# ScalarE makes each scan step's decay half a step later in its order

## The reference, cut to what matters

```
def step(ht, inp):
    x_t, dt_t, B_t, C_t = inp
    dA = jnp.exp(dt_t[..., None] * A)
    dB = dt_t[..., None] * B_t[:, None, :]
    ht = dA * ht + dB * x_t[..., None]
    y_t = jnp.sum(ht * C_t[:, None, :], axis=-1)
    return (ht, y_t)
```

## Time and profile before

| what | us |
|---|---|
| median of 3 runs (lowest, highest) | 2696.54 (2693.64, 2705.16) |
| the profiled execution, its own time | 2710.37 |
| its span | 2708.3 |
| busy: PE, DVE, ACT, POOL | 2271.3 (84%), 1850.7 (68%), 1767.2 (65%), 1738.4 (64%) |

### The profile page before, as it was taken

The page is one execution under the profiler, slowest core; times in us unless marked ns, Lnnn a source line. Parts: engine busy times, 40 slices in busy tenths (PEclk is TensorE's granted clock), DMA queues, the critical chain, the costliest instruction groups (busy, mean ns, idle before and its releaser), DMA issues.

```text
span 2708.3 us, 38199 instructions
## 1 busy us (share of the span) xinstructions
PE 2271.3 (84%) x13192; PEld 1417.2 (52%) x13192; DVE 1850.7 (68%) x2832; ACT 1767.2 (65%) x3278; POOL 1738.4 (64%) x1416
## 2 busy tenths in 40 slices
PE   5777879999688889799989898989888988987781
PEld 4444557775444456455644465546544644554351
DVE  5778544543246786687578766876777667788888
ACT  3556534446277876788677867785887677766762
POOL 1000254425757997788788879876987797655565
PEclk9888989999899999999989998999999999998895
DMA  4000258874555676555665475447543844476776
GB/s 158 24 20 6 88 156 237 235 219 77 102 110 120 129 154 155 110 115 122 162 122 103 111 167 115 100 104 172 111 100 84 191 105 86 94 172 151 172 183 143
DMA packets 282032, 344.50 MB, mean 127 GB/s; under 512 B 66159, under 2 KB 211504, under 8 KB 281840
## 3 DMA queue, kind: packets, MB, share of 16 engines
q0 software_dynamic: 84080, 175.67, 34.7%
q1 hardware_dynamic: 175248, 144.83, 18.2%
q10 hardware_dynamic: 22512, 21.57, 2.4%
HBM read 198.26 MB, written 26.80 MB: 83 GB/s over the span
## 4 chain that ended last, share of the span: by engine, by line
PE 26%; POOL 15%; issue 11%; DVE 10%; ACT 9%; DMA 1%; POOLq 0%; DVEq 0%; SPq 0%; ACTq 0%
POOL arena L1661 6%; PE bank L1913 4%; PE bank L1944 4%; POOL acc_sb L1639 4%; DVE bank L1536 4%; POOL arena L1667 3%; POOL arena L1677 2%; PE bank L1739 2%; PE bank L1786 2%; PE bank L1779 2%; PE bank L1836 2%; PE bank L1798 2%; ACT Pr L1043 2%; DVE arena L1502 1%; ACT bank L1160 1%
## 5 line engine op out<-in xcount | busy, mean ns | idle before, releaser
L1661 POOL TENSOR_TENSOR arena<-arena 128x512 f32<-128x512 f32 x512 | 874.3, 1785 | 18.2 <-DVE arena L1527 9.5
L1639 POOL DMA_INDIRECT acc_sb<-ybuf,slot_idx x256 | 422.5, 1650 | 132.6 <-DMA ybuf<-arena 60.8
L1252 DVE TENSOR_REDUCE negmax<-bank 128x1 f32<-128x512 f32 x512 | 339.8, 680 | 240.8 <-PE bank L1779 239.2
L1160 ACT ACTIVATE bank<-arena,A_sb 128x512 f32<-128x512 f32 x512 | 353.4, 694 | 149.8 <-DVE arena L1541 131.2
L1043 ACT ACTIVATE Pr<-bank,negmax 128x512 f32<-128x512 f32 x512 | 358.5, 700 | 135.1 <-DVE negmax L1252 133.6
L1667 POOL TENSOR_TENSOR arena<-arena 128x512 f32<-128x512 f32 x192 | 297.5, 1550 | 231.5 <-DVE arena L1536 231.2
L1536 DVE TENSOR_TENSOR_SCAN bank<-bank,arena 128x512 f32<-128x512 f32 x320 | 390.0, 1219 | 67.1 <-ACT bank L1160 61.2
L1786 PE MATMUL bank<-ident,Pr 128*128 128x128 f32 x2048 | 341.1, 291 | 79.2 <-ACT PT L1025 77.5
L1786 PEld LDWEIGHTS bank<-ident,Pr 128*128 128x128 f32 x2048 | 229.1, 145 | 317.6 <-ACT PT L1025 181.1
L1025 ACT COPY PT<-bank 128x512 f32<-128x512 f32 x512 | 303.3, 592 | 128.6 <-PE bank L1786 101.0
L1779 PE MATMUL bank<-Kp,Qp 64*128 64x512 f32 x1024 | 301.5, 666 | 70.9 <-ACT Pr L1043 59.2
(11 more groups left out here) (216 smaller groups left out, 3773.7 us busy)
## 6 DMA issues: line engine op xcount, KB each, us to landing
arena<-arena POOLq DMA_DIRECT2D x255, 512.0 KB, 5.3
arena<-bc_dram SPq DMA_DIRECT2D x256, 256.0 KB, 3.8
ybuf<-arena ACTq DMA_DIRECT2D x64, 256.0 KB
arena<-in_w_gate SPq DMA_DIRECT2D x64, 128.0 KB
arena<-in_w_up SPq DMA_DIRECT2D x64, 128.0 KB
arena<-in_w_down SPq DMA_DIRECT2D x64, 128.0 KB
arena<-in_X SPq DMA_DIRECT2D x8, 512.0 KB, 8.4
s_sb<-in_X SPq DMA_DIRECT2D x8, 512.0 KB
```

The costliest lines, as they stand in the source:

```text
L1160: act.activation(bank[DECAY[g % 2]][:, :], dt_sb[:, size_slot(b, cb), :], ACT.Exp, scale=A_sb[:, cb, n:n + 1]).then_inc(ssm_decay, 1)
L1252: dve.tensor_reduce(negmax[:, m % RING_STAT:m % RING_STAT + 1], bank[m % RING_S_ATT][:, :], AX.X, ALU.max, negate=True).then_inc(att_max, 1)
L1639: pool.indirect_dma_start(acc_sb[:, i, :], None, ybuf, bass.IndirectOffsetOnAxis(ap=slot_idx[:, b * TILES + i, k:k + 1], axis=0), bounds_c ...
L1661: pool.tensor_tensor(st_sb[:, g % RING_S, :], u_sb[:, size_slot(b, cb), :], B_sb[:, load % RING_BC, :], ALU.mult).then_inc(ssm_input, 1)
```

## The change

The method `decay` of ScalarE becomes `ssm_step` itself, and its `ssm_mid` goes. Before, decay g + 1 was written in `ssm_mid(g)`, in the middle of step g (and decay 0 at step 0). Now decay g is written at the start of step g. The conditions it waits for are the same.

```
                 ins.then_inc(ssm_soft, 1)
 
             def ssm_step(self, g):
-                if g == 0:
-                    self.decay(0)
-
-            def ssm_mid(self, g):
-
-                self.decay(g + 1)
-
-            def decay(self, g):
                 if g < NB * SCAN:
                     b, cb, n, _ = ssm_place(g)
                     w.wait_ge(ssm_dt, len(SIZE_PARTS) * b + PART_OF[cb] + 1)
```

## The result

| | median us | lowest, highest | runs |
|---|---|---|---|
| before | 2696.26 | 2691.47, 2705.16 | 9 |
| after | 2714.65 | 2712.0, 2728.55 | 9 |

The ratio is 1.0069, with a 95% interval of [1.0053, 1.0086]: the change makes the kernel 18.4 us slower, more than the 0.5% that the prediction took as the bound of what can be told. The time lies inside the range of 2684 to 2727; the likeliest case, no change, did not come.

What follows compares the result with a forecast made beforehand. PE was taken to bound tree stretches, VectorE the last stretch, and no single engine attention. The terms +1 + 2 + 7 - 7 gave +3 us, a median of 2699.5, said as 2700, with a range of 2684 to 2727.

Steps and rivals of the forecast that it cites:

- no change: Whole kernel: the time stays within 0.5%, 2683 to 2710 us; chance some 0.45.
- slower rival: Attention: VectorE stands in line behind the late decay, so row maxima and GpSimd's product are late; 2727 us, chance 0.36.
- The sum, +3: Whole kernel: the four parts, +1 + 2 + 7 - 7, in us.
- Part 1: Tree stretches of batches 3, 4 and 5: six more table loads at 1.28 us, mostly covered; +1 us, bounds 0 and 7.7.
- the worked place: Trees of batch 5: two more loads make a silu late and cost PE 0.3 us.
- Part 2: Last stretch: eight decays fall behind a silu pair and stall scans; +2 us, bounds -2 and +15.
- Part 3: Attention: scans wait longer for the later decay, 54 us on VectorE, an eighth taken; +7 us, bounds 0 and +27.
- Part 4: Mainly attention: most of ScalarE's 60.9 us idling for VectorE before decays goes; -7 us, bounds 0 and -30.
- its mark: Outside the last stretch: scans' waits for the decay rise from 62.3 us to 90 or more.
- I am wrong if attention stretches grow by over 3 us each: Attention: the prediction's own sign of failure, by which VectorE's line behind late decays would be the story.
- The faster rival: ScalarE's idling for the product by C held up PE; 2676.5 us if half goes through, 2686.5 if a third; chance 0.19.
- the banks fix the decay's time whatever the order says: Whole kernel: the two banks set when a decay runs, so the order changes nothing; 2697.5 us, chance 0.10.

Runs made afterwards that it cites:

- e5: Kernel before with only three decays (steps 148, 212, 276) made later, enough to bring the six more table loads; ratio 0.9995.
- e3: Kernel before with decays later only in the tree stretches of the first six batches (111 decays, 183 table loads); ratio 1.0017.
- e4: Kernel before with decays later only in the last stretch, from scan step 409 on (103 decays); ratio 1.0018.
- e2: Kernel before with decays later only in the attention stretches (298 decays); ratio 1.0034.
- e7: Kernel before with decay g + 1 at the start of step g, half a step earlier; ratio 1.0111.
- f3: Changed order, with a third decay buffer in SBUF and an input ring of eight slots instead of ten; ratio 1.0421 against the kernel before.
- f2: Kernel before, order kept, with a third decay buffer in SBUF and an input ring of eight slots instead of ten; ratio 1.0341.
- e6: Decay g in the middle of step g, a whole step later than in the kernel before; ratio 1.0677.
- f1: Kernel before with an input ring of eight slots instead of ten, still two decay banks; ratio 0.9990.
- e1: The changed kernel itself, unedited, built and timed again against the kernel before; ratio 1.0071.

## Why the prediction was off, step by step

The measured time lies in the range only because the range reached up to the slower rival. The sum, +3, was 15 us short, and no change was the likeliest case.

**Part 1, table loads (+1).** The loads alone cost nothing that can be told in the time (e5). At the worked place PE idled 0.57 us for 0.3 foretold. By length the three stretches grew by 5.2 us in e5, five times the term, which the other stretches of that execution gave back.

**Trees without loads: no term.** The sum had nothing for the other decays in the tree stretches, since PE is full there. e3 measures the trees at +4.6 us, loads included, and the scans' waits for decays in them grew by 42.3 us (61.1 to 103.4). PE being full 62.27 of 63 us in one stretch is not PE full in all: between their scans the six tree stretches of before have PE busy 86 to 93% of the time. The waits had been there to see: summed by stretch, 61.1 of the 62.3 us in which scans waited for decays before lie in tree stretches. Whether the +4.6 is these decays or the loads is open, as said with e5.

**Part 2, last stretch (+2).** The mechanism was right, down to the place (0.80 us for 0.9) and to the waits (30.6 us, foretold between 22 and 35). The size was not: e4 has +4.9, from six decays and not eight. The working gave "+5 if VectorE carries all of it", and it does, as an engine busy 86% of the stretch would; I took 2 for what earlier trees might give back, and no row had shown that they would.

**Part 3, attention, the later decay (+7).** Its working was not what happened. It put 54 us of added waits on the 36 scans that waited already and took these to be in attention; only two of them are, with 1.2 of their 62.3 us. In e2 the attention's waits for decays grow by 35.3 us (1.2 to 36.5), nearly all at scans that had made it before, like the one worked through. About a quarter of that is what reaches the end, +9.2, after whatever part 4 gave back.

**Part 4, the other side (-7).** This is the step that failed. "Of the 60.9 us that ScalarE idled, most goes" was wrong: 45.0 remained, where under 25 was foretold. So was "much of the idling is in tree stretches": by stretch it was 12.7 us in trees, of which 3.0 are left, and 55.5 in attention, of which 48.6 are. Nearly all of those in attention stand in six bunches, one at the end of each attention stretch (decays 61 to 65, 129 to 132, 198 to 202, 266 to 273, 335 to 339 and 404 to 408), and the largest are the same in both kernels: 4.6 us at decay 201, 4.2 at 337, 7.5 and 7.7 at 271. There VectorE is late by several us, and half a step makes no odds. What the fall by 15.9 us was worth is not measured by itself. At the third of a us that e7 pays for each it would be 5 to 6 us, an estimate, and the 23 us that f3 loses against f2, for 18.4 of the change, would allow as much; but in attention, where the gain was to be, only 6.9 us of idling went. The second half of the part, decays vanishing in ScalarE's waits for the maximum (69.8 us), shows nowhere: those are 68.5 after.

By stretch the measured parts are 4.6 (trees) + 4.9 (last) + 9.2 (attention) = 18.7, for a sum of 1 + 2 + 0 = 3. Of the 15.7 between them 9.2 is attention, where parts 3 and 4 were to cancel and did not, 3.6 the trees and 2.9 part 2. How the 9.2 splits into a price of part 3 and a gain of part 4 no run shows.

**The rivals.** The slower one had the sign and the engine, and its mark came true (the scan's waits rose to 134.3, with 90 or more foretold). Its price, 27 us for attention alone, was some three times what e2 has: VectorE's slack on the scores carried most of it (153.5 to 125.6 us in e2), the very argument against it. "I am wrong if attention stretches grow by over 3 us each" did not come either: in e2 they grew by 1.8 on average (10.8 over six), and the loss is spread thinly, 0.03 us for each decay moved in attention, 0.04 in trees, 0.05 in the last stretch. The faster rival finds little for it: not much bank waiting went, and what went bought less than the later decays cost. That the banks fix the decay's time whatever the order says is refuted, since the order alone costs up to 6.8%.

What weighed wrongly was treating both waits as equals because their sums were near each other (60.9 and 62.3 us). The one is paid by whoever stands behind a decay on ScalarE, the other by VectorE, and through it by the maximum and GpSimd's product. Either can reach the time (e7 and e6); the half step moved much of the one and little of the other.

No version was measurably faster than before; f1 comes nearest with 0.9990 [0.9978, 1.0003].

## What to carry to other kernels

A producer between a buffer's release and a consumer's need has a best place in a hand-written order; price the two sides by what stands behind the waiting instruction on each engine, not by the sums of waiting. Half a step of lateness is cheap only while the consumer's engine has slack elsewhere (here 153.5 us of waiting for scores); look at how much is left, since here the second half step cost ten times the first. Where a stretch has an engine at 86% and no other wait to absorb a stall, count the whole stall, and check each stretch before writing that a full engine covers it. Before a difference between two single executions is given to the code, look at the granted clock of just that stretch: in one tree stretch of e3, 3.4 us at the lower level made half of what had looked like a cost of late decays. And sum a wait by stretch before giving it to one: a total over all of them had put both waits of this case in the wrong place.

## What the hardware showed

The third decay buffer cost 3.4% by where it lies. VectorE in f2, by form (count, then busy us and mean ns of one):

```profile
L1537 DVE TENSOR_TENSOR_SCAN arena<-arena 128x512 f32<-128x512 f32 x170 | 350.6, 2062 | 31.2 <-ACT arena L1161 25.8 <-POOL arena L1662 5.4
...
L1537 DVE TENSOR_TENSOR_SCAN bank<-bank,arena 128x512 f32<-128x512 f32 x214 | 260.5, 1217 | 21.4 <-ACT bank L1161 19.6 <-POOL arena L1662 1.8
...
L1542 DVE TENSOR_TENSOR arena<-bank,arena 128x512 f32<-128x512 f32 x214 | 147.9, 691 | 7.3
L1542 DVE TENSOR_TENSOR arena<-arena 128x512 f32<-128x512 f32 x106 | 120.6, 1138 | 3.6
```

The same scan with both inputs in SBUF takes 2062 ns on average, with the decay in PSUM 1217; the product 1138 and 691. That is 170 x 0.845 + 106 x 0.447 = 191 us more of VectorE's busy time, about its whole rise, from 1850.7 to 2042.2 us. It is not the instruction's own length: 64 of the 170 took under 1.26 us, among them all 41 that no product of GpSimd overlapped. A long one, VectorE and GpSimd of f2:

```profile
972.09 1.87 POOL L1668 TENSOR_TENSOR arena<-arena 128x512 f32<-128x512 f32 x1
...
972.79 2.26 DVE L1537 TENSOR_TENSOR_SCAN arena<-arena 128x512 f32<-128x512 f32 x1
```

GpSimd's product was over at 973.96, and the scan at 975.05, 1.09 us after it, as if it had begun only then. Of the 95 scans of this kind that started while a product of GpSimd was under way, 59 ended 1.08 or 1.09 us after the end of that product, and 35 of the others later still. The 156 scans with the decay in PSUM that started so took at most 1.232 us. GpSimd's own products kept their length (1765 ns in f2, 1775 in f1). The Trainium skill (SBUF — State Buffer, Who interferes with whom) states that a VectorE instruction with two inputs in SBUF contends with a GpSimd instruction that reads SBUF, and that the order of issue decides which of them blocks. The trace agrees with the first, with the 1.09 us above. The second it does not bear out in full: 20 more of these scans are recorded as starting 0.02 to 0.75 us before a product, and they too ended 1.09 us after the end of one, while the input products that started during such a scan took 1774 ns on average, like all of them (1765). The blocked time is shown in the rows as the instruction's busy time, so it is found by its mean and not in the waits. Whether this alone makes the 3.4% was not tried by itself.

The mean granted clock of an execution goes with its time, by as much as most of the experiments here cost. Of the nine timed executions of after, seven with a mean clock of 0.944 to 0.947 took 2712.0 to 2715.0 us, and the two with 0.938 took 2721.9 and 2728.6; of the six of e1, the same kernel, the one with 0.947 took 2707.9 us and the two lowest, 0.939 and 0.940, 2722.1.
